# Low halves of the cross attention's context on GpSimd, and VectorE's row maximum behind its subtraction

## What is computed

```python
q = (query @ wq.T + bq).reshape(B, SQ, H, HD).transpose(0, 2, 1, 3)
k = (key @ wk.T + bk).reshape(B, -1, H, HD).transpose(0, 2, 1, 3)
v = (value @ wv.T + bv).reshape(B, -1, H, HD).transpose(0, 2, 1, 3)
scores = jnp.einsum('bhqd,bhkd->bhqk', q, k) / jnp.sqrt(jnp.asarray(HD, q.dtype))
attn = jax.nn.softmax(scores, axis=-1)
ctx = jnp.einsum('bhqk,bhkd->bhqd', attn, v)
```

## Time and profile before

| | us |
|---|---|
| median of 3 runs | 1724.16 |
| lowest and highest of them | 1718.86, 1724.18 |
| the profiled execution | 1722.41 |
| its span, first to last instruction | 1720.6 |

### The profile page before, as it was taken

One profiled execution on the slowest core, in us unless ns is written; L12 is line 12 of the kernel. 1 busy time (PEld: TensorE's weight loads), 2 busy tenths in 40 slices (PEclk: granted clock), 3 DMA queues, 4 the chain that ended last, 5 costly groups with the idle time before them and its releaser, 6 DMA issues. The chain is left out here.

```text
span 1720.6 us, 36999 instructions
## 1 busy us (share of the span) xinstructions
PE 1618.0 (94%) x15604; PEld 1310.2 (76%) x15604; DVE 1264.2 (73%) x1643; ACT 941.5 (55%) x1437; POOL 676.6 (39%) x352
## 2 busy tenths in 40 slices
PE   7999999999999999999999999768899799999999
PEld 6777777777777777777777777657787677777787
DVE  5248998999899899989998997877633577753322
ACT  4347666766666766666666666653201777631000
POOL 0004565655556555556555566102000244432210
PEclk9999999999999999999999999879899899899999
DMA  5322222222222222222222220213323111211001
GB/s 183 75 43 39 35 37 37 35 35 40 38 37 37 37 35 35 37 36 36 36 41 34 37 37 7 77 48 114 135 86 99 62 50 50 64 50 49 25 25 50
DMA packets 310404, 88.75 MB, mean 52 GB/s; under 512 B 259392, under 2 KB 292160, under 8 KB 310240
## 3 DMA queue, kind: packets, MB, share of 16 engines
q1 hardware_dynamic: 310240, 86.39, 21.7%
HBM read 71.67 MB, written 14.68 MB: 50 GB/s over the span
## 5 line engine op out<-in xcount | busy, mean ns | idle before, releaser
L650 POOL TENSOR_TENSOR b_acc<-b_acc,b_s 128x1024 f32<-128x1024 f32 x168 | 462.5, 2753 | 250.6 <-ACT b_s L843 243.6
L923 DVE TENSOR_TENSOR b_mx<-b_psS,b_mx 128x512 f32<-128x512 f32 x480 | 328.1, 684 | 26.4 <-PE b_psS L709 13.3
L888 DVE TENSOR_TENSOR b_s<-b_s,b_mb 128x2048 f32<-128x2048 f32 x128 | 340.8, 2664 | 3.2 <-ACT b_mb L826 3.2
L860 ACT ACTIVATE b_s<-b_psS 128x2048 f32<-128x2048 f32 x128 | 241.0, 1883 | 150.4 <-DVE b_mx L923 150.4
L843 ACT ACTIVATE b_s<-b_s 128x2048 f32<-128x2048 f32 x128 | 245.3, 1916 | 68.4 <-DVE b_s L888 68.4
L43 PE MATMUL b_work<-wvT,cT 128*128 128x512 f32 x496 | 203.0, 409 | 0.0
L43 PE MATMUL b_work<-cT,wkT 128*128 128x512 f32 x496 | 200.3, 404 | 1.7 <-POOL b_ones L636 1.7
L709 PE MATMUL b_psS<-b_q,b_kT 32*128 32x128 f32 x4096 | 153.9, 287 | 47.6 <-ACT b_s L860 47.5
L44 PE MATMUL b_work<-wvT,cT 128*128 128x512 f32 x496 | 194.5, 392 | 0.0
L44 PE MATMUL b_work<-cT,wkT 128*128 128x512 f32 x496 | 194.2, 392 | 0.0
L45 PE MATMUL b_work<-wvT,cT 128*128 128x512 f32 x496 | 193.8, 391 | 0.0
(11 more groups left out here) (290 smaller groups left out, 2780.8 us busy)
## 6 DMA issues: line engine op xcount, KB each, us to landing
cin<-in_ctx SPq DMA_DIRECT2D x480, 64.0 KB, 2.3
experts_sb<-in_L_ffn_expert_w SPq DMA_DIRECT2D x8, 1024.0 KB, 5.4
q_scratch<-d_st SPq DMA_DIRECT2D x16, 256.0 KB, 2.3
k_scratch<-d_st SPq DMA_DIRECT2D x16, 256.0 KB, 2.3
e_q<-q_scratch SPq DMA_DIRECT2D x16, 256.0 KB, 2.7
k_sb<-k_scratch SPq DMA_DIRECT2D x16, 256.0 KB, 2.9
cin<-in_ctx SPq DMA_DIRECT2D x4, 512.0 KB, 8.5
b_kT<-in_x SPq DMA_DIRECT2D x4, 512.0 KB, 8.1
```

The lines of the kernel that those rows point to most:

```text
L650: nc.gpsimd.tensor_tensor(acc[:, :, :], acc[:, :, :], s[:, buf, 2 * i:2 * i + 2, :], ALU.add).then_inc(sum_done, 1)
L860: nc.scalar.activation(s[:, n % BUFS, :, :].rearrange("p t (j q) -> p t j q", j=HG), psS[:, :, :].rearrange("p j (t q) -> p t j q", t=CHUN ...
L888: nc.vector.tensor_tensor(s[:, n % BUFS, :, :], s[:, n % BUFS, :, :], mb[:, :].rearrange("p (o n) -> p o n", o=1).broadcast_to([P, CHUNK, ...
L923: nc.vector.tensor_tensor(mx[:, :, :], part, mx[:, :, :], ALU.max).then_inc(mx_done, 1)
```

## The change

The subtraction that makes the low half of a quarter goes from VectorE's program into GpSimd's, in the same beat, ahead of that beat's sums. It still waits for `hi_done` and still raises `split_done`. Beside it, VectorE's row maximum (`top`, once in a slot) goes behind the subtraction of `mb` in the same beat.

```diff
@@ block.gpsimd
             nc.gpsimd.memset(ones[:, :], 1.0).then_inc(const, 1)
-            for n in range(TAIL * CHUNK):
+            def context_lo(p, k):
+                pool.wait_ge(hi_done, p * CHUNK + k + 1)
+                nc.gpsimd.tensor_tensor(cT[1][:, p % 2, k, :], cin[:, 1, k % 2, :], f32(cT[0][:, p % 2, k, :]),
+                                        ALU.subtract).then_inc(split_done, 1)
+
+            def sums(n):
                 m, c = divmod(n, CHUNK)
...
+            for beat in range(FIRST, LAST):
+                if (x0 := transposed(beat)) is not None:
+                    context_lo(*x0)
+                if (n := exp_step(beat)) is not None and n < TAIL * CHUNK:
+                    sums(n)
@@ block.vector
             for beat in range(FIRST, LAST):
-                if (m := spread_slot(beat)) is not None:
-                    i, bank = RING["M", m, 0], work[BANK["M", m, 0]]
-                    dve.wait_ge(work_full, i + 1)
-
-                    reached(dve, spread_done, m - 1)
-                    nc.vector.tensor_reduce(top[:, m % 2, :], bank[:, :].rearrange("p (j k) -> p j k", j=HG),
-                                            AX.X, ALU.max).then_inc(top_done, 1)
                 if (n := exp_step(beat)) is not None:
...
                         ALU.subtract).then_inc(sub_done, 1)
+                if (m := spread_slot(beat)) is not None:
+                    i, bank = RING["M", m, 0], work[BANK["M", m, 0]]
+                    dve.wait_ge(work_full, i + 1)
+
+                    reached(dve, spread_done, m - 1)
+                    nc.vector.tensor_reduce(top[:, m % 2, :], bank[:, :].rearrange("p (j k) -> p j k", j=HG),
+                                            AX.X, ALU.max).then_inc(top_done, 1)
...
-                if (x0 := transposed(beat)) is not None:
-                    p, k = x0
-                    dve.wait_ge(hi_done, p * CHUNK + k + 1)
-                    nc.vector.tensor_tensor(cT[1][:, p % 2, k, :], cin[:, 1, k % 2, :], f32(cT[0][:, p % 2, k, :]),
-                                            ALU.subtract).then_inc(split_done, 1)
                 if (x0 := turned_next(beat)) is not None:
                     context_turned(*x0)
```

## The result

The changed kernel takes 1691.76 us in the median of 4 runs (1690.80 to 1692.03), beside 1723.07 us for the kernel before (1718.86 to 1724.18, 4 runs): ratio 0.9822, 95% interval 0.9804 to 0.9840. The forecast was 1690.8 us, with a range of 1685 to 1706. It holds, but as the sum of two errors: the cross attention won more than was forecast, and a later stage that the change doesn't touch gave back more than that.

What follows compares the result with a forecast made beforehand. It took TensorE, busy 94% of the span, to bound the kernel, with waits for ScalarE's move to win: 1722.41 - 34.4 + 1.0 = 1689.0 us profiled, plus 1.75 for the median, 1690.8 us; range 1685 to 1706.

Steps and rivals of the forecast that it cites:

- the followed chain: Beat 32's scores wait 1.24 us, traced through move, maxima and beat 30's low half, stalled until GpSimd's sum ends.
- the order: Subtraction of `mb` ahead of `top` in beat 28: `top` up to 0.8 us late, 2.5 us of cover, so 0.
- -34.4 us for the waits: All 31 waits of TensorE's scores for ScalarE's move, from 100 to 1060 us, go: 34.4 us won.
- GpSimd's low half at 1.28: Price of one low half on GpSimd, taken from an addition of the same size: 1.28 us, ends 1.15 and 2.4.
- The spare times: Margins ahead of TensorE's need: 0.7 us at beat 30's move, 4.4 us at the fourth chunk's sums for the denominators.
- The lock's turns: GpSimd's sums and VectorE's instructions with two SBUF inputs exclude each other, one whole instruction at a time, and alternate.
- Rivals B and C: B: GpSimd keeps the lock through two sums in beat 30, 1704 us, chance 0.17; C: likewise beat 28, 1761 us, 0.05.
- the maxima of 513.11: VectorE's maxima in the followed slot, one input in PSUM, took 2.82 us; cited beside the lock's rule.
- +1.0 us in the last slot: `top` comes 1.4 us later there, less 0.3: spread, L754 and last outputs about 1.0 us later.
- Rival D: GpSimd's loop per slot, 26.3 us plus three low halves, becomes the bound: 1717 us, chance 0.06.
- Later stages: Stages behind the cross attention had no term in the forecast sum.
- a fall of the clock: Sign of being wrong: a granted clock below 1.00 between 200 and 1000 us, which no row can exclude.

Runs made afterwards that it cites:

- e4: Kernel before, with six of a slot's seven GpSimd sums cut to 128x16 elements and low halves still on VectorE: 1686.58 us, ratio 0.9797.
- e1: Kernel before with only VectorE's order changed, the subtraction of `mb` ahead of `top`, low halves still on VectorE: 1702.19 us, ratio 0.9871.
- e2: Kernel before with only the low halves moved to GpSimd, `top` still ahead of the subtraction: 1685.90 us, ratio 0.9790.
- e3: Changed kernel with each low half made twice on GpSimd: 1769.49 us, ratio 1.0263.
- e5: Changed kernel with VectorE's old order, `top` ahead of the subtraction, in the last four slots only: 1686.04 us, ratio 0.9792.
- e6: Changed kernel with 8 matmuls that do nothing added at the start of self attention: 1690.21 us.
- e9: Kernel with low halves on GpSimd and VectorE's old order, plus 8 added matmuls at the start of self attention: 1691.83 us.

## Why the prediction was right, point by point

- **What bounds it, and the followed chain: right.** Move, maxima, low half, GpSimd's sum. e4 shows it by taking away only the sums. What was not seen is that the chain had a second weak link: e1 undoes most of the stall by another way, 28 of 38.8 us, since `top`'s gap ahead of the subtraction made the sums late. The prediction gave the order a 0 in the even slots, which is right for the sum of both edits (e2) and would have been wrong for that edit alone.
- **-34.4 us for the waits: 4.4 us too small.** By its scores, the cross attention became 38.8 us shorter. The list of waits gives 1.24 us for an even slot, but the slots shrank by 33.73 - 32.42 = 1.31 us, since the list leaves out small gaps beside the wait; over 25 even slots that is 1.8 us. Of the other 2.6, 0.7 lie in the first three slots, which shrank by 3.3 us where the list has 2.6, and 1.8 in the last two, behind the 1060 us at which the list ended. What shortened those two was not followed.
- **GpSimd's low half at 1.28: measured 1.30.** The nearest row of the same size was the right one to take. It is 1.9 times the 0.69 us of VectorE, and the move wins all the same, since GpSimd's work is not on the path.
- **The spare times: right.** 0.7 us at the move of beat 30, measured 0.8; 4.4 us at the denominators, measured 501.77 - 489.83 - 6.79 = 5.2.
- **The lock's turns: right.** In the timelines read, no subtraction had to wait for both sums of a chunk (the longest of all lasted 4.1 us, 1.8 more than alone). Rivals B and C did not come. `top` stands behind a subtraction of 3.77 us and TensorE doesn't wait for it. One support of the reading was weaker than it looked: the maxima of 513.11, said to be free of the lock at 2.82 us, ran while GpSimd idled. The same slot has others with a sum running all through them (520.73 to 525.65), and they show it:

```profile
521.48 2.82 DVE L923 TENSOR_TENSOR b_mx<-b_psS,b_mx 128x512 f32<-128x512 f32 x4
```

- **+1.0 us in the last slot: measured 0.9.** The wait ahead of L765 is 2.68 us in place of 1.80:

```profile
1121.06 1.09 PE L765 MATMUL b_work<-ident,b_spread 128*128 128x128 f32 x4 [2.68 <-ACT b_spread L849]
```

- **Rival D's loop: wrong by what it left out.** It named `acc` as what TensorE would wait for and had three low halves in it. e3 shows that four belong there and that the wait is for `cT`, 50.0 us in all. Its chance was also added up loosely: half of 0.06 on either side gives 0.05 for same and 0.05 for slower, where 0.04 and 0.06 stand.
- **Later stages: not in the sum at all.** The step that failed is the silent one, that what lies behind the cross attention keeps its length: +4.9 us in self attention, and 1.3 of the 2.3 us around the stages (1.0 was forecast, for the last slot). The prediction named a fall of the clock as a danger, but within 200 to 1000 us, where it stayed at 1.00. The total came out near the forecast by luck: the two errors, 4.4 us won and 6.2 lost, leave the profiled execution at 1690.8 us, 1.8 above the 1689.0 forecast for it. The median is off by 1.0 only, since it lies 0.96 us above its profiled execution, where 1.75 had been added.

## What to carry to other kernels

VectorE with two inputs in SBUF and GpSimd exclude each other instruction by instruction; what counts is not either engine's load but which of the two sits at the lock when a short step on the path comes by, so move the short step off VectorE, or move the long ones away in time, and try each edit of a pair alone. Add up the lock's load per period, with everything that meets there, before giving GpSimd more: idle time that a profile shows on GpSimd is not all free. When a change shortens a stage, look at the stages behind it for a changed clock before crediting or blaming the edit: here a shift of under two microseconds was worth five. The versions with the low halves on GpSimd and the old order kept at least in the last slots (e2 and e5, 1686 us) owe most of their lead over the changed kernel to that.

## What the runs showed of the hardware that was not expected

- The granted clock's pattern in one stage has two forms that differ by 4.9 us, and small shifts of the stage's start, 1.7 us of added matmuls, turn one into the other, both ways (e6, e9). In twelve profiles the first stretch at the lower clock begins 4.3 to 4.4 or 6.0 to 6.3 us after the stage's first scores, never between. The form mostly repeats from run to run, so it looks like a property of the kernel: the 9 runs of the changed kernel lie at 1690.8 to 1693.5 us, and both that have a profile show the slow form.
- A queue of GpSimd's instructions did not shut VectorE out: in all the timelines read, the waiting subtraction got the lock when GpSimd's running instruction ended, even with another right behind it (3.20 us for a subtraction of 2.28 that came during a sum).
- An instruction of VectorE with one input in PSUM does not take part in the lock: four maxima took 2.82 us while GpSimd idled (513.11) and 2.82 while it made sums throughout (521.48).
